# A recurrent block on one core: another loading order and another order of the first products, in the start of the kernel

## The reference, cut to what matters

```python
xn = _layernorm(x)                                  # mean and variance of each row, eps 1e-5
K = _s4_kernel(Lambda, p, q, Vc @ Bp, Ct, step, 512)
s = irfft(rfft(xn, 1024) * rfft(K, 1024), 1024)[..., :512] + D[0] * xn   # causal convolution along the columns
h1 = xn @ w1.T + (xn @ A1.T) @ B1.T * 2             # 512 -> 1376, low-rank term of rank 16
h3 = xn @ w3.T + (xn @ A3.T) @ B3.T * 2
g  = silu(h1) * h3
f  = g @ w2.T + (g @ A2.T) @ B2.T * 2               # 1376 -> 512
out = x + s * silu(f)
```

## Time and profile before

| | us |
|---|---|
| median of 3 runs | 412.18 |
| lowest and highest | 411.95 and 412.45 |
| the profiled execution | 412.45 |
| its span (first to last instruction) | 410.7 |
| PE busy | 404.4 (98%) |
| DVE busy | 164.6 (40%) |
| ACT busy | 107.2 (26%) |
| POOL busy | 67.4 (16%) |

### The profile page before, as it was taken

One profiled execution on the slowest core, in us unless ns is written; L12 is line 12 of the kernel. 1 busy time (PEld: TensorE's weight loads), 2 busy tenths in 40 slices (PEclk: granted clock), 3 DMA queues, 4 the chain that ended last, 5 costly groups with the idle time before them and its releaser, 6 DMA issues.

```text
span 410.7 us, 5004 instructions
## 1 busy us (share of the span) xinstructions
PE 404.4 (98%) x1856; PEld 337.3 (82%) x1856; DVE 164.6 (40%) x259; ACT 107.2 (26%) x176; POOL 67.4 (16%) x130
## 2 busy tenths in 40 slices
PE   8899999999999999999999999999999999999996
PEld 7888888888888888888888888888888888888885
DVE  5877785654693321233244222132334212211125
ACT  7553323322441111122222111212122111111122
POOL 5327627340700114000000101400000000000000
PEclk9999999999999999999999999999999999999999
DMA  8563942220416101000005201000002000000002
GB/s 264 154 234 91 318 131 79 76 96 22 153 51 207 51 2 51 2 0 0 0 29 197 84 0 51 0 0 0 0 0 102 2 0 0 2 0 0 2 0 102
DMA packets 14338, 26.20 MB, mean 64 GB/s; under 512 B 2560, under 2 KB 4608, under 8 KB 14320
## 3 DMA queue, kind: packets, MB, share of 16 engines
q1 hardware_dynamic: 13872, 24.85, 18.7%
q0 software_dynamic: 160, 0.59, 0.4%
q10 hardware_dynamic: 288, 0.52, 0.4%
HBM read 20.33 MB, written 4.53 MB: 61 GB/s over the span
## 4 chain that ended last, share of the span: by engine, by line
PE 95%; DVE 2%; DMA 1%; SPq 1%; issue 0%; DVEq 0%
PE h L934 20%; PE h L935 20%; PE h L936 20%; PE f L935 10%; PE f L934 10%; PE f L936 10%; PE h L957 2%; PE spare L921 1%; DMA xn<-x_dram 1%; PE spare L916 1%; PE spare L936 1%; PE spare L935 1%; PE spare L934 1%; PE spare L1063 0%; DVE xres L815 0%; DVE rows_next L812 0%
## 5 line engine op out<-in xcount | busy, mean ns | idle before, releaser
L934 PE MATMUL h<-xt,w 128*128 (+2 forms) x340 | 131.5, 387 | 0.0
L935 PE MATMUL h<-xt,w 128*128 (+2 forms) x340 | 131.1, 386 | 0.0
L936 PE MATMUL h<-xt,w 128*128 (+2 forms) x340 | 131.1, 386 | 0.0
L936 PEld LDWEIGHTS h<-xt,w 128*128 128x128 f32 x340 | 63.9, 188 | 12.8
L934 PEld LDWEIGHTS h<-xt,w 128*128 128x128 f32 x340 | 63.9, 188 | 12.7
L935 PEld LDWEIGHTS h<-xt,w 128*128 128x128 f32 x340 | 63.9, 188 | 12.6
L796 DVE TENSOR_TENSOR g<-g,h 128x512 f32<-128x512 f32 x40 | 27.5, 688 | 111.6 <-PE h L936 111.6
L801 DVE TENSOR_TENSOR ghl<-g,ghl 128x512 fp32r<-128x512 f32 x44 | 31.6, 719 | 92.5 <-ACT ghl L625 92.5
L934 PE MATMUL f<-ghl,w2f 128*128 128x512 f32 x176 | 68.6, 390 | 0.0
L935 PE MATMUL f<-ghl,w2f 128*128 128x512 f32 x176 | 68.5, 389 | 0.0
L625 ACT CAST ghl<-g 128x512 fp32r<-128x512 f32 x44 | 27.3, 621 | 157.7 <-PE f L936 144.7
(11 more groups left out here) (131 smaller groups left out, 303.7 us busy)
## 6 DMA issues: line engine op xcount, KB each, us to landing
raw<-w_dram SPq DMA_DIRECT2D x28, 256.0 KB, 3.6
xres<-xT_dram SPq DMA_DIRECT2D x4, 1024.0 KB, 7.2
outT_dram<-xres SPq DMA_DIRECT2D x15, 256.0 KB, 2.4
rows_next<-x_dram SPq DMA_DIRECT2D x4, 512.0 KB, 3.7
scale_rows<-scales_scratch SPq DMA_DIRECT2D x3, 512.0 KB, 4.1
rows<-x_dram SPq DMA_DIRECT2D x2, 512.0 KB, 8.3
raw<-w_dram SPq DMA_DIRECT2D x4, 224.0 KB, 2.5
lora_stack<-lora_spread_split SPq DMA_DIRECT2D x3, 204.0 KB, 3.8
```

The costliest lines, as they stand in the source:

```text
L934: pe.matmul(out, w[1], m[0], start=start, stop=False)
L935: pe.matmul(out, w[0], m[1], start=False, stop=False)
L936: return pe.matmul(out, w[0], m[0], start=False, stop=stop)
```

## The change

The start of the kernel is written in another order on all engines, and one more fold is done in it:

- SP: raw(1,0) is loaded ahead of the wait for the cleared factors; row tile 3 and raw(3,0) ahead of the two spread loads; the trig table and raw(2,1) ahead of the copies of the stack. raw(2,0) keeps its place.
- The plain factors take in those of fold (2,0): the load grows from 1536 to 2176 columns on 16 partitions, and VectorE clears 1216 of them instead of 832, GpSimd 960 instead of 704.
- Fold (2,0) moves from tile 1's gate place into the start, fold (3,3) from tile 2's up place to tile 1's down place; the table for j == 2 is gone, since the general rule gives the other two.
- TensorE: 11 products in keep_busy instead of 9; another order of folds and turns, with turns 2 and 3 behind the first products of h1; fold (2,0) ahead of the second half of the rows; B as two products with weights of 64 rows, one column each, instead of one with 128 rows and two columns.
- VectorE: the adds of (1,1) and (3,1) stand ahead of the lows of row tiles 2 and 3; the add and the low of (2,0) come at the end of the start. ScalarE: the order of its casts follows, and the cast of (2,0) precedes silu 0.
- The Toeplitz block is cast at tile 8 instead of tile 9. GpSimd makes its low half between the two rstd steps of block 1. The trig table shares the semaphore of the other state inputs, so GpSimd's first step waits for it too.

```diff
-FIRST_COLS = {1: 2 * D, 3: 2 * D + 2 * P}
-LORA_FIRST = 2 * D + 4 * P
+FIRST_COLS = {1: 2 * D, 3: 2 * D + 2 * P, 2: 2 * D + 5 * P}
+LORA_FIRST = 3 * D + 5 * P
...
-FACTORS_BY_DVE = 832
-PLAIN = {1: 1, 3: 1, 2: -1}
-A_FIRST = {1: 0, 3: D}
...
-FOLD_FIRST = [(1, 0), (3, 0), (1, 1), (3, 1)]
+FACTORS_BY_DVE = 1216
+PLAIN = {1: 1, 3: 1, 2: 0}
+A_FIRST = {1: 0, 3: D, 2: 2 * D + 4 * P}
...
+FOLD_FIRST = [(1, 0), (3, 0), (1, 1), (3, 1), (2, 0)]
...
     if j == 1:
-        return {"gate": [(2, 0), (1, 2)], "up": [(3, 2), (1, 3)], "down": [(2, 1)]}[place]
-    if j == 2:
-        return {"gate": [(1, 4)], "up": [(3, 3), (3, 4)], "down": [(2, 2)]}[place]
+        return {"gate": [(1, 2)], "up": [(3, 2), (1, 3)], "down": [(2, 1), (3, 3)]}[place]
...
-TOEPLITZ_AT = (9, "up")
+TOEPLITZ_AT = (8, "up")
...
             load_tile(0)
+            load_raw(1, 0)
             sync.wait_ge(factors_dve, 1)
             sync.wait_ge(factors_pool, 1)
             sync.dma_start(lr[0:P:STACK_STEP, :], lora).then_inc(lora_in, 16)
             sync.dma_start(lane_c[:, :], lanes).then_inc(const_in, 16)
-            load_raw(1, 0)
+            load_tile(3)
+            load_raw(3, 0)
             sync.dma_start(spread[:, 0:LANES_ST], lora_st).then_inc(spread_in, 16)
             sync.dma_start(spread[:, LANES_ST:LANES_ST + LANES_MV], lora_mv).then_inc(spread_in, 16)
-            load_tile(3)
-            load_raw(3, 0)
-            for kind, j in FOLD_FIRST[2:] + [(2, 0)]:
+            for kind, j in FOLD_FIRST[2:]:
                 load_raw(kind, j)
             sync.dma_start(lane_d[:, :], s4_lanes).then_inc(s4_in, 16)
             sync.dma_start(scal[:, :], s4_scalars.to_broadcast([P, 2])).then_inc(s4_in, 16)
             sync.dma_start(bp_sb[:, :], s4_bp).then_inc(bvec_in, 16)
             sync.dma_start(vc_sb[:, :], s4_vc).then_inc(bvec_in, 16)
+            sync.dma_start(trig_sb[:, :, :].rearrange("p a l -> p (a l)"), trig.to_broadcast([P, 2 * D])) \
+                .then_inc(s4_in, 16)
+            load_raw(2, 1)
...
-            early = [(1, 2), (3, 2), (1, 3), (2, 1), (3, 3)]
-            for kind, j in early[:2]:
-                load_raw(kind, j)
-            sync.dma_start(trig_sb[:, :, :].rearrange("p a l -> p (a l)"), trig.to_broadcast([P, 2 * D])) \
-                .then_inc(trig_in, 16)
-            for kind, j in early[2:]:
+            early = [(1, 2), (3, 2), (1, 3), (3, 3)]
+            for kind, j in early:
                 load_raw(kind, j)
             sync.dma_start(dft_sb[:, :, :], dft).then_inc(dft_in, 16)
-            later = [f_ for f_ in FOLDS[len(FOLD_FIRST):] if f_ not in early + [(2, 0)]]
+            later = [f_ for f_ in FOLDS[len(FOLD_FIRST):] if f_ not in early + [(2, 1)]]
...
             rows_norm(1)
+            rows_hi(0)
             fold_hi(1, 0)
-            rows_hi(0)
+            rows_hi(1)
+            fold_hi(3, 0)
             act.wait_ge(spread_in, 32)
             nc.scalar.copy(spread_hl[:, 0, :], spread[:, :]).then_inc(spread_hi, 1)
             rows_norm(2)
-            rows_hi(1)
             rows_norm(3)
-            fold_hi(3, 0)
             rows_hi(2)
+            fold_hi(1, 1)
             rows_hi(3)
-            fold_hi(1, 1)
             fold_hi(3, 1)
+            fold_hi(2, 0)
             hidden(0, 0)
...
             fold_add(1, 0)
             rows_first(3)
             fold_add(3, 0)
+            rows_lo(0)
             fold_lo(1, 0)
-            rows_lo(0)
+            rows_lo(1)
             dve.wait_ge(spread_hi, 1)
             nc.vector.tensor_tensor(spread_hl[:, 1, :], spread[:, :], spread_hl[:, 0, :].bitcast(F32), ALU.subtract) \
                 .then_inc(spread_lo, 1)
-            rows_lo(1)
             fold_lo(3, 0)
+            fold_add(1, 1)
+            fold_add(3, 1)
             rows_lo(2)
             rows_lo(3)
-            fold_add(1, 1)
-            fold_add(3, 1)
             fold_lo(1, 1)
             fold_lo(3, 1)
+            fold_add(2, 0)
+            fold_lo(2, 0)
             hidden_mul(0, 0)
...
-                if (kind, j) == FOLDS[len(FOLD_FIRST)]:
+                if (kind, j) == (1, PLAIN[1] + 1):
...
-                keep_busy(9)
+                keep_busy(11)
                 pe.wait_ge(lora_in, 16)
                 fold(1, 0)
-                fold(3, 0)
                 pe.wait_ge(const_in, 16)
                 turn_rows(0)
+                fold(3, 0)
+                turn_rows(1)
                 fold(1, 1)
-                turn_rows(1)
-                fold(3, 1)
-                turn_rows(2)
                 pe.wait_ge(whi_done, 1)
                 pe.wait_ge(xhi_done, RT // 2)
                 for c in range(DC):
                     pe.matmul(h1[:, lo], w13_tile(1, 0, 0)[:, c, :], xt[:, 0, 0, c, lo], start=(c == 0), stop=False)
-                turn_rows(3)
+                fold(3, 1)
                 wait_split(pe, 1, 0)
                 pe.wait_ge(xlo_done, RT // 2)
                 for c in range(DC):
                     pe.matmul(h1[:, lo], w13_tile(1, 0, 1)[:, c, :], xt[:, 0, 0, c, lo], start=False, stop=False)
                     pe.matmul(h1[:, lo], w13_tile(1, 0, 0)[:, c, :], xt[:, 0, 1, c, lo], start=False, stop=(c == DC - 1))
+                turn_rows(2)
+                turn_rows(3)
                 wait_split(pe, 3, 0)
                 hidden(0, 0, 0, 3, h3, lo)
+                fold(2, 0)
                 pe.wait_ge(xlo_done, RT)
                 hidden(0, 0, 0, 1, h1, hi).then_inc(h1_ready, 1)
                 bankt = take(0, ("B",), True)
                 pe.wait_ge(bvec_in, 32)
-                pe.matmul(bankt[:, 0:2], vc_sb[:, :], bp_sb[:, :], start=True, stop=True).then_inc(b_ready, 1)
+                for ri in range(2):
+                    mm = pe.matmul(bankt[:, ri:ri + 1], vc_sb[:, ri * P:(ri + 1) * P], bp_sb[:, :], start=True, stop=True)
+                mm.then_inc(b_ready, 1)
                 hidden(0, 0, 0, 3, h3, hi).then_inc(h3_ready, 1)
...
-            pool.wait_ge(s4_in, 16 * 2)
+            pool.wait_ge(s4_in, 16 * 3)
...
             rows_rstd(1, 0)
-            rows_rstd(1, 2)
             pool.wait_ge(tz_hi, 1)
             tt(tzs[:, 1, :], tz[:, :], tzs[:, 0, :].bitcast(F32), ALU.subtract).then_inc(tz_lo, 1)
-            pool.wait_ge(tz_lo, 1)
+            rows_rstd(1, 2)
...
-    vct = vc.transpose(2, 1, 0).reshape(2 * NS, NS)
-    vct = _np.concatenate([vct, vct], axis=1)
-    bp = _np.asarray(L0_attn_Bp)
-    no = _np.zeros_like(bp)
-    bp = _np.concatenate([_np.concatenate([bp, no]), _np.concatenate([no, bp])], axis=1)
+    vct = vc.transpose(1, 2, 0)
+    vct = _np.concatenate([vct[:, 0], vct[:, 0], vct[:, 1], vct[:, 1]], axis=1)
```

More of the change, by code:

```diff
@@ L279, in build @@
         scales = put("scales", [P, 2, RT])
-        bp_sb = put("bp_sb", [P, 2])
+        bp_sb = put("bp_sb", [NS, 1])
         scal = put("scal", [P, 2])
@@ L308, in build @@
         even_odd = put("even_odd", [P, 2, D // 2])
-        vc_sb = put("vc_sb", [P, P])
+        vc_sb = put("vc_sb", [NS, 2 * P])
         krow = put("krow", [P, P + D])
@@ L347, in build @@
         spread_in, stack_in, stack_cleared = sem("spread_in"), sem("stack_in"), sem("stack_cleared")
-        s4_in, trig_in, bvec_in, dft_in = sem("s4_in"), sem("trig_in"), sem("bvec_in"), sem("dft_in")
+        s4_in, bvec_in, dft_in = sem("s4_in"), sem("bvec_in"), sem("dft_in")
         res0_in, res_in = sem("res0_in"), sem("res_in")
@@ L659, in body @@
                         if first and (j, place) == (1, "gate"):
-                            act.wait_ge(trig_in, 16)
+                            act.wait_ge(s4_in, 16 * 3)
                             act.wait_ge(small_ready, 1)
@@ L1335 @@
         "w1": c(turned_tiles(L0_ffn_w1)), "w3": c(turned_tiles(_np.asarray(L0_ffn_w3)[up])), "w2": c(_np.asarray(L0_ffn_w2).T),
-        "lora": _np.concatenate([a1, a3, b1.T[:, :2 * P], b3.T[:, :2 * P]], axis=1),
+        "lora": _np.concatenate([a1, a3, b1.T[:, :2 * P], b3.T[:, :2 * P], a2[:, :P], b2.T], axis=1),
         "lora_st": lora_st.reshape(P, LANES_ST),
         "lora_mv": lora_mv.reshape(P, LANES_MV),
-        "s4_lanes": c(lanes_d), "s4_vc": c(vct), "s4_bp": c(bp),
+        "s4_lanes": c(lanes_d), "s4_vc": c(vct), "s4_bp": c(_np.asarray(L0_attn_Bp)),
         "s4_scalars": c(_np.stack([_np.asarray(L0_attn_D), _np.asarray(L0_attn_log_step)], axis=1)),
```

## The result

| | us, median | lowest to highest | ratio, 95% interval | profiled span |
|---|---|---|---|---|
| before, same chip | 412.45 | 411.95 to 413.16 | | 410.7 |
| after | 414.84 | 414.69 to 415.17 | 1.0056 [1.0042, 1.007] | 413.3 |

The account below looks back on a forecast made before the run. Bound: TensorE's gapless stream, its start, its matmuls and an untouched tail. Terms +0.26 (second half), +0.24 (B), −0.23 (fold) sum to +0.27 us on the 412.18 median: 412.45, written 412.4; range 411.6 to 413.2.

Parts of the forecast that it names:

- Things with the same answer ... All cost 0: Moved loads, stack copies, GpSimd's small chain, denominators, Toeplitz cast and later rstd: each in time or off the path, 0 us.
- no other wait until the end: Sign of being right: after its waits before the second half of the rows, TensorE has none; any after 20 us excluded.
- Folds (3,3) and (1,2) only change place in it: In TensorE's gapless stream these two folds move without changing its length: no cost.
- B: Before tile 1 on TensorE: two products with 64-row weights instead of one add 0.24 us, bounds 0 and 0.24.
- Loading order: At the start, row tile 3 lands earlier, so VectorE begins its statistics at 8.25 instead of 9.07: gain 0.82 us.
- rival B: At the start, raw(1,0) in flight delays row tile 0 by 0.7 us: 413.2; chance 0.11.
- C: Rival at the start: reordered loads bring nothing, tile 3 still lands at 9.04; sum +1.09, 413.3; chance 0.04.
- VectorE's order: Two adds, 1.75 us together, ahead of row low 3: it ends at 16.48, the second half starts +0.26 us later.
- rival A: VectorE less late before the second half, adds 0.60 each or not the bound: 411.7 to 411.9; chance 0.22.
- The 0.75 that TensorE would wait before the second half: TensorE, done with fold (2,0) at 15.88, arrives 0.75 us before VectorE's row low 3 lets it go on.
- ScalarE: Before tile 1: cast of (2,0) ends at 18.95, silu 0 at 19.5, needed at 19.97; free, 0.45 in hand.
- The fold that left: Fold (2,0) leaves TensorE's gapless stream at tile 1's gate place: −0.23 us.

Follow-up runs that it names:

- e6: The kernel before with only the Toeplitz cast moved to tile 8: 413.43 us, ratio 1.0016.
- e1: The changed kernel with the Toeplitz cast back at tile 9 and GpSimd's order around it as before: 414.19 us, ratio 1.0033.
- e3: The changed kernel with fold (2,0) back at tile 1's gate place, from the stack factors, with its add, cast and low half: 414.01 us, ratio 1.0025.
- e8: The changed kernel with ScalarE's three denominator steps at tile 1's down place instead of its gate place: 418.67 us, ratio 1.014.
- e11: The changed kernel with Toeplitz back at tile 9 (GpSimd's old order), B as one product, fold (2,0) at its old place from the stack: 412.98 us, ratio 1.0005.
- e15: e14 with the trig table and raw(2,1) loaded behind the copies of the stack: 412.40 us, ratio 0.9989.
- e2: The changed kernel with the trig table loaded behind the stack copies again, on its own semaphore: 414.67 us, ratio 1.0039.
- e16: The kernel before with only VectorE's adds of (1,1) and (3,1) moved ahead of the lows of row tiles 2 and 3: 413.64 us, ratio 1.0016.
- e12: e11 with VectorE's lows of row tiles 2 and 3 back ahead of the adds of (1,1) and (3,1): 412.54 us, ratio 0.9996.
- e5: e11 with ScalarE's denominators at tile 1's down place: 417.72 us, ratio 1.0116.
- e10: e5 with VectorE's lows of row tiles 2 and 3 ahead of the adds of (1,1) and (3,1): 417.99 us, ratio 1.0116.
- e14: e12 with the small plain factors of before and raw(1,0) loaded behind row tile 3: 412.52 us, ratio 0.9993.

## Why the prediction was wrong

**The step that failed** is "Things with the same answer ... All cost 0". It asked of each moved step whether its result came in time. It did not ask whom the step meets. The Toeplitz cast was indeed long possible and nobody waited for it, but the split behind it fell on a low half that TensorE wanted at once: +0.56 here, +0.58 in e6, the wait gone in e1. The denominators on GpSimd, "off the path", fell on the low half of (1,2): +1.04, gone in e3 and e8. Together 1.60 of the 2.58, and with it "no other wait until the end" fell. The text itself had called any wait after 20 us a sign that it was wrong.

A second sentence belongs to it: "Folds (3,3) and (1,2) only change place in it". The held low half made the add of (1,3) end at 30.53, and fold (3,3) needs its bank. At its old place the next fold behind (2,1) would have come 2.96 later (29.07 to 32.03 in the kernel before), near 32.8, when that bank had long been free. So I estimate from these starts that the meeting costs TensorE something only together with the new place of (3,3), 0.23 behind (2,1). No run has the meeting with (3,3) at its old place; e3, e8 and e11 have the new place with VectorE not held, and no wait.

The forecast was +0.27. To the 2.58 are missing: 1.60 for the two meetings, 0.27 at the start of the second half, 0.26 for B, and 0.05 and 0.14 that belong to no term.

What put the denominators there: in the earlier trace rows fold (2,0) was 0.23 us of TensorE, and I took that as the whole of it. It was also an add and a cast ahead of them. Against tile 1 GpSimd began 8.86 after in the kernel before, 6.69 with the change, 7.44 in e3, and 8.42 in e15, where trig is late as well. VectorE's low half came at 7.04, 6.81, 7.03 and 7.61. The change is the only one of the four where GpSimd is ahead. With trig in time it is fold (2,0) that sets the place: 6.69 in e2, where trig is late, as in the change, and 7.45 in e16, the kernel before with trig in time, as in e3. In the kernel before ScalarE also waited 1.31 for trig. The rest between e3 and e15 is only in part trig: ScalarE waited 0.32 for it, and fold (2,0) came 0.48 later behind tile 1, because of the stack.

The Trainium skill (SBUF — State Buffer, section Who interferes with whom) says that a VectorE instruction with two SBUF inputs contends with a GpSimd instruction that reads SBUF. That whoever issues first has the shared ports for its whole instruction it says of VectorE's two-port modes. The traces show both for this plain float32 subtraction: 0.68 to 1.73 where GpSimd led by 0.12, 0.68 unchanged where VectorE led by 0.41. I had not applied the rule to any moved step. The trace of before held the evidence too: the low half at 28.84, beside GpSimd's step from 28.33, took 1.33.

**Loading order: right.** Row tile 3's statistics began at 8.49 (8.25 foreseen) with no wait; tile 0's at 4.01, so rival B did not occur, nor C (whose 9.04 for the landing is 9.07 in the earlier trace rows). One part was short: the larger factors landed late, fold (1,0) started at 6.38, not 5.5, and VectorE idled 0.21. That is the 0.24 by which row low 1 ended late (12.37 against 12.13).

**VectorE's order: right in mechanism and price.** Row low 3 ended at 15.45 + 1.29 = 16.74 (16.48 foreseen, the 0.24 again). e16 has the 1.76. This refutes rival A. The Trainium skill's sentence (VectorE: DVE Perf Modes, section The DRAIN you can't avoid) that a semaphore after each instruction costs nothing extra does not hold here, where VectorE waits for the semaphore of its own add before it goes on: 1.76 for two adds, not 1.20.

**The 0.75 that TensorE would wait before the second half: wrong, without effect.** Fold (2,0) took 15.85 to 16.80, 0.95 instead of 0.23, and ended in a tie with row low 3. e3 shows the wait of 0.78 that it covered. The second half came at +0.43 (forecast +0.26), and another 0.10 at its first products, which after a plain-factor fold come 0.22 apart instead of 0.12.

**ScalarE: right.** The cast of (2,0) ended at 19.19 and silu 0 at 19.69, before tile 1 at 20.49, and TensorE never waited for ScalarE there.

**B: right in sign, half of the size.** +0.50, not +0.24, in two kernels. The bounds 0 and 0.24 rested on weight loads alone; with 64 rows and one column each the two products took 0.73 against 0.23, four records instead of two.

**The fold that left: −0.23, right as a term.**

## What to carry to other kernels

Of every step that is moved, ask three things: is its input there, who waits for its result, and which instruction on the neighbouring engine will run at that moment; a trace that shows the same operation once at 0.68 and once at 1.33 is telling where two engines meet. A term taken out of TensorE's stream also takes its cast and add out of the queues of the other engines, and shifts all that stands behind them. A product that is moved forward gives up the slack it had before its bank was wanted. A wait just found should be measured by start times in a run that leaves it out, and its repair should be looked at for who is queued behind the step that is delayed. Behind a long wait of TensorE look at the granted clock too.

## What the hardware showed that I had not expected

- The meeting is decided by who starts first: 0.04 or 0.12 us of lead for GpSimd cost VectorE 1.05 to 1.11 us; a lead of 0.41 for VectorE cost GpSimd 0.13. The second one ends later by the overlap less some 0.13 to 0.15: VectorE's 0.68 ended 0.55 after GpSimd's step, and GpSimd lost 0.13 of an overlap of 0.27 in e3 and 0.17 of 0.32 in e12.
- After TensorE had waited 3.0 to 3.3 us in e5, e8 and e10, its granted clock was 0.50 for 3.4 us. In e8 this cost 1.71 us beside the wait itself, in e5 and e10 I did not work it out.
- In one execution of e15 TensorE's products came at half pace until 10.3 us, in the others until 3.9 to 6.3. That execution reached tile 1 1.12 us later than the one of e14.
- A 512-column fold product from plain factors took 0.95 us from start to start (two records), from split factors 0.23 to 0.24.
- Two products of one column with 64-row weights took 0.73 us of TensorE where one of two columns with 128 rows took 0.23.
- Row tile 3 of the unchanged load order landed at 8.63 in one execution and 9.07 in another, which moves the start of the stream by 0.4 us: a single profile can hide an edit of that size.
